# Building a scaled adjacency matrix quarter by quarter, with ScalarE's and VectorE's order in the first two pairs written anew

## The reference, cut to what matters

```
h    = relu(layernorm(x))                        # over the 1024 nodes
S    = normalised mean of h over the batch       # 1024 nodes x 128 features
sim  = (S S^T + 1) / 2
A    = (sim + g0 > 1 - sim + g1)                 # 1024 x 1024, zeros and ones
M    = clip(A + A^T + I, 0, 1);  C = M M^T       # common neighbours
W    = A * (C / max C * C)  where valid
deg  = W.sum(axis=0);  dinv = deg^-0.5 (0 where deg = 0)
Wn   = dinv[:,None] * W * dinv[None,:]
out  = x + (sum over s of Wn[s,d] * (h @ adj)[s]) + bias
```

## Time and profile before

| | us |
|---|---|
| median of 3 executions | 867.53 (867.31 to 867.67) |
| the profiled execution | 867.24 |
| its span, first to last instruction | 865.5 |
| TensorE busy with matmuls | 825.9 (95%) |
| VectorE busy | 582.5 (67%) |
| ScalarE busy | 507.1 (59%) |
| mean granted TensorE clock | 0.988 |

### The profile page before, as it was taken

The page is one execution under the profiler, slowest core; times in us unless marked ns, Lnnn a source line. Parts: engine busy times, 40 slices in busy tenths (PEclk is TensorE's granted clock), DMA queues, the critical chain, the costliest instruction groups (busy, mean ns, idle before and its releaser), DMA issues.

```text
span 865.5 us, 13587 instructions
## 1 busy us (share of the span) xinstructions
PE 825.9 (95%) x4771; PEld 431.2 (50%) x4778; DVE 582.5 (67%) x669; ACT 507.1 (59%) x522; POOL 314.8 (36%) x255
## 2 busy tenths in 40 slices
PE   4999999968899999999999999999999999999997
PEld 3544455544354555455545545555555455545553
DVE  7999987789846665666566556655665666566652
ACT  3888705877636664556456556656665655465531
POOL 4888810035004333433333333333333433333320
PEclk9999999997899999999999999999999999999999
DMA  8999903100643222222333333222222222222111
GB/s 334 409 410 357 421 13 122 49 1 1 236 154 98 98 98 98 98 97 97 97 126 108 111 111 125 98 97 97 97 97 97 97 97 97 97 97 98 60 63 73
DMA packets 30122, 113.15 MB, mean 131 GB/s; under 512 B 3472, under 2 KB 3600, under 8 KB 29072
## 3 DMA queue, kind: packets, MB, share of 16 engines
q1 hardware_dynamic: 30096, 112.80, 36.1%
HBM read 79.23 MB, written 33.55 MB: 130 GB/s over the span
## 4 chain that ended last, share of the span: by engine, by line
PE 77%; DVE 10%; issue 4%; ACT 4%; POOL 3%; DMA 0%; POOLq 0%; DVEq 0%; ACTq 0%; SPq 0%
PE ps L811 65%; PE ps L761 8%; DVE stats L903 4%; PE ps L779 1%; POOL rstd L335 1%; DVE a L1072 1%; DVE xring L1066 1%; POOL zbuf L345 1%; PE ps L690 1%; ACT zbuf L403 0%; ACT xring L574 0%; ACT a L579 0%; PE ps L704 0%; DVE moments L909 0%; ACT hring L454 0%
## 5 line engine op out<-in xcount | busy, mean ns | idle before, releaser
L811 PE MATMUL ps<-a,ybuf 128*128 128x512 f16 x2604 | 573.6, 380 | 3.4 <-ACT obuf L501 3.4
L811 PEld LDWEIGHTS ps<-a,ybuf 128*128 128x128 f16 x2604 | 253.2, 98 | 301.1 <-ACT obuf L501 3.9
L991 DVE TENSOR_TENSOR ybuf<-zbuf,ybuf 128x1024 f16<-128x1024 f32 x124 | 163.9, 1321 | 165.7 <-ACT ybuf L487 165.7
L371 POOL TENSOR_TENSOR zbuf<-zbuf 128x512 f32<-128x512 f32 x31 | 39.8, 1284 | 452.3 <-ACT zbuf L468 452.3
L487 ACT ACTIVATE ybuf<-zbuf 128x1024 f16<-128x1024 f32 x124 | 117.6, 950 | 110.4 <-POOL zbuf L376 97.2
L501 ACT ACTIVATE obuf<-ps,bias_sb,w_out 128x512 f32<-128x512 f32 x62 | 47.9, 773 | 126.6 <-PE ps L811 126.6
L980 DVE TENSOR_TENSOR hring<-hring 128x1024 f16<-128x1024 f32 x56 | 68.6, 1224 | 55.8 <-ACT hring L454 55.8
L761 PE MATMUL ps<-w,hring 128*128 128x128 f16 x1344 | 85.4, 221 | 11.6 <-DVE hring L980 9.8
L761 PEld LDWEIGHTS ps<-w,hring 128*128 128x128 f16 x1344 | 80.6, 99 | 24.8 <-DVE hring L980 10.1
L1138 DVE TENSOR_TENSOR obuf<-obuf,xring 128x1024 f32<-128x1024 f32 x64 | 78.3, 1225 | 2.7
L374 POOL TENSOR_TENSOR zbuf<-zbuf 128x512 f32<-128x512 f32 x31 | 70.4, 2271 | 0.0
(11 more groups left out here) (132 smaller groups left out, 675.0 us busy)
## 6 DMA issues: line engine op xcount, KB each, us to landing
xring<-in_x_dram SPq DMA_DIRECT2D x96, 512.0 KB, 4.7
out_dram<-obuf SPq DMA_DIRECT2D x64, 512.0 KB, 2.9
ybuf<-in_x_dram SPq DMA_DIRECT2D x28, 512.0 KB, 8.4
a<-in_L_gnn_gumbel_dram SPq DMA_DIRECT2D x7, 1024.0 KB, 14.7
obuf<-in_x_dram SPq DMA_DIRECT2D x11, 512.0 KB, 5.3
obuf<-in_L_gnn_gumbel_dram SPq DMA_DIRECT2D x1, 1024.0 KB, 22.7
w<-in_adj_dram SPq DMA_DIRECT2D x1, 64.0 KB, 1.8
bias_sb<-in_L_gnn_bias_dram SPq DMA_DIRECT2D x1, 0.5 KB, 2.2
```

Of the source, the lines that this page charges most:

```text
L811: mm = nc.tensor.matmul(bank[q % 2], y16[:, q % 2, yk, u, c * P:(c + 1) * P], a16[:, ak, mat, c, :], start=(start and c == yk == ak == 0), ...
L991: nc.vector.tensor_tensor(y16[:, q % 2, 1, a:a + n, :], z[:, a + 1:a + 1 + n, :], y16[:, q % 2, 0, a:a + n, :], ALU.subtract).then_inc(s_y, 1)
```

## The change

- `rooted` and `square` work on halves of 512 columns, 16 instructions each instead of 8 and 8, in the order of the quarters (rows_hi LO, rows_hi HI, rows_lo LO, rows_lo HI). ScalarE squares a quarter (4 instructions) and copies it at once; VectorE's `low` of a quarter stands behind the `rooted` of the next one.
- The bounds and roots of the degrees stand ahead of `y_low(0, 1, 2)`; `y_low(0, 1, 2)` and `y_low(0, 1, 3)` move behind the `low` of block 2. `relu2` is cut in its two activations, with `degree_of(7)` between those of entry 4.
- On TensorE q is spread in two halves, the first ahead of `turn(1)`. The fourteen `stay_awake` behind the last mask become five, and eight more stand behind the first block's `high`, ahead of the first product. `xw_of(0, 2, 1)` moves from there into pair 1, which now runs with its look-ahead.
- ScalarE's and VectorE's lists for pairs 0 and 1 are written out: the block results of pair 0 (`first_out`), `relu2(0, 3, 0)` and the work for pair 2 stand between the copies of the sums; `upper0(0, 1)` and `upper1(0, 1)` and two `y_low` stand ahead of pair 0's `add_x`.
- The masked counts lie in other slots of the matrix buffer.

```diff
-        masked = [tile16(e // 4, 5 + e // 2 % 2, e % 2) for e in range(C)]
+        masked = [tile16(half, mat, k) for half, mat in ((0, 5), (1, 5), (1, 3), (1, 4)) for k in (0, 1)]
...
             degree_of(6)
+            relu2_wide(0, 2, 0)
             degree_of(7)
+            relu2_high(0, 2, 0)
             y_high(0, 1, 3)
-            relu2(0, 2, 0)
...
+            def square(rows, k, half, c):
+
+                if k == 0 and half == 0 and c == 0:
+                    act.wait_ge(s_kap, 3)
+                act.wait_ge(s_e, C * k + HC * half + c + 1)
+                r = rows[:, c, half * H:(half + 1) * H]
+                nc.scalar.activation(r, r, ACT.Square, scale=kappa[:, 0:1]).then_inc(s_a32, 1)
...
+            for n, (mat, rows, k, half) in enumerate(((0, rows_hi, 0, 0), (A12, rows_hi, 0, 1),
+                                                      (1, rows_lo, 1, 0), (2, rows_lo, 1, 1))):
+                for c in range(HC):
+                    square(rows, k, half, c)
+                act.wait_ge(s_a32, HC * (n + 1))
+                high(mat, rows[:, :, half * H:(half + 1) * H])
             relu2(0, 2, 1)
...
             act.wait_ge(s_t, 1)
             high(3, spare)
+            act.wait_ge(s_wout, 1)
+            act.wait_ge(s_hhi, 5)
+            first_out(0)
+            relu2(0, 3, 0)
+            first_out(1)
+            z_of(0, 2, 0)
             act.wait_ge(s_t, 2)
             high(4, rows_hi[:, :, LO])
+            first_out(2)
+            first_out(3)
+            y_high(0, 2, 0)
+            act.wait_ge(s_hhi, 6)
+            partial(0, 1, 0)
             act.wait_ge(s_t, 3)
             high(5, rows_hi[:, :, HI])
-            relu2(0, 3, 0)
+            partial(0, 1, 1)
             act.wait_ge(s_t, 4)
             act.wait_ge(s_mm, 14 + 3)
             high(6, spare)
...
+            partial(0, 1, 2)
+            z_of(0, 2, 1)
+            y_high(0, 2, 1)
             relu2(0, 3, 1)
-            act.wait_ge(s_hhi, 7)
-            act_pair(0, 1, True, False, False)
+            y_high(0, 2, 2)
+            y_high(0, 2, 3)
...
             pe.wait_ge(s_m, C)
-            stay_awake(ps[:, 3, 0:P], 14)
-            turn(1)
-            spread(1)
+            stay_awake(ps[:, 3, 0:P], 5)
...
+            pe.wait_ge(s_adjt, C)
+            pe.wait_ge(s_q, 2)
+            q_row(0)
+            turn(1)
+            q_row(1)
+            spread(1)
             xw_of(0, 2, 0)
-            xw_of(0, 2, 1)
+            pe.wait_ge(s_ahi, 1)
+            stay_awake(ps[:, 3, 0:P], 8)
...
-                if ahead1:
+                if ahead1 and not second:
                     xw_of(i, q + 1, 0)
...
-            pe.wait_ge(s_e, C)
-            pe_pair(0, 1, False, True)
+            pe.wait_ge(s_e, 2 * C)
+            pe_pair(0, 1, True, True)
...
             mask(7)
-            y_low(0, 1, 2)
             root(0, 0, 6)
             bound(1, 6, C)
             root(1, 6, C)
...
+            h_low(0, 2, 0)
+            dve.wait_ge(s_qrow, 1)
+            rooted(rows_hi, 0, 0, 0)
             top_of(1)
-            y_low(0, 1, 3)
+            rooted(rows_hi, 0, 0, 1)
...
+            rooted(rows_hi, 0, 0, 2)
+            rooted(rows_hi, 0, 0, 3)
...
-            h_low(0, 2, 0)
             dve.wait_ge(s_qrow, 2)
             for c in range(HC):
-                rooted(rows_hi, 0, c)
+                rooted(rows_hi, 0, 1, c)
+            low(0, 0, rows_hi[:, :, LO])
             for c in range(HC):
-                rooted(rows_lo, 1, c)
+                rooted(rows_lo, 1, 0, c)
+            low(1, A12, rows_hi[:, :, HI])
+            for c in range(HC):
+                rooted(rows_lo, 1, 1, c)
+            low(2, 1, rows_lo[:, :, LO])
+            dve.wait_ge(s_a32, C)
+            nc.vector.tensor_tensor(spare, rows_hi[:, :, HI], rows_hi[:, :, LO], ALU.subtract).then_inc(s_t, 1)
+            low(3, 2, rows_lo[:, :, HI])
             h_low(0, 2, 1)
...
+            y_low(0, 1, 2)
+            y_low(0, 1, 3)
             dve.wait_ge(s_t, 1)
             dve.wait_ge(s_alo, 2)
             nc.vector.tensor_tensor(rows_hi[:, :, LO], rows_lo[:, :, HI], spare, ALU.subtract).then_inc(s_t, 1)
+            low(4, 3, spare)
+            low(5, 4, rows_hi[:, :, LO])
             nc.vector.tensor_tensor(rows_hi[:, :, HI], rows_lo[:, :, HI], rows_hi[:, :, HI],
                                     ALU.subtract).then_inc(s_t, 1)
-            low(4, 3, spare)
             dve.wait_ge(s_t, 2)
             dve.wait_ge(s_alo, 5)
             nc.vector.tensor_tensor(spare, rows_lo[:, :, LO], rows_hi[:, :, LO], ALU.subtract).then_inc(s_t, 1)
-            low(5, 4, rows_hi[:, :, LO])
+            h_low(0, 3, 0)
             low(6, 5, rows_hi[:, :, HI])
-            h_low(0, 3, 0)
             low(7, 6, spare)
...
+                if isinstance(i, int) and r == 1:
+                    dve.wait_ge(s_hhi, BODY - 1)
...
+            upper0(0, 1)
+            y_low(0, 2, 0)
+            upper1(0, 1)
+            y_low(0, 2, 1)
             add_x(0, 0, 0)
             add_x(0, 0, 1)
             h_low(0, 3, 1)
-            dve_pair(0, 1, True, False)
+            y_low(0, 2, 2)
+            lower0(0, 1)
+            add_x(0, 1, 0)
+            y_low(0, 2, 3)
+            lower1(0, 1)
+            add_x(0, 1, 1)
```

More of the change, by code:

```diff
@@ L432, in _, with relu2_wide @@
                                      accum_out=row_count[:, c:c + 1]).then_inc(s_mask[0], 1)
-            def relu2(i, q, b):
+            def relu2_wide(i, q, b):
                 i, q = i + q // PAIRS, q % PAIRS
                 j = 2 * q + b
-                if j == RESIDENT:
-                    return
                 n = (BODY - 1) * i + j - 1
@@ L451, in relu2, with relu2_high @@
                 t = BODY * i + j
-                bias, scale = nbias[:, bass.ds(t, 1)], rstd[:, bass.ds(t, 1)]
-                nc.scalar.activation(h32, src, ACT.Relu, bias=bias, scale=scale).then_inc(s_h32, 1)
-                nc.scalar.activation(h16[b][:, 0, :], src, ACT.Relu, bias=bias, scale=scale).then_inc(s_hhi, 1)
+                nc.scalar.activation(h32, src, ACT.Relu, bias=nbias[:, bass.ds(t, 1)],
+                                     scale=rstd[:, bass.ds(t, 1)]).then_inc(s_h32, 1)
+            def relu2_high(i, q, b):
+                i, q = i + q // PAIRS, q % PAIRS
+                j = 2 * q + b
+                first = isinstance(i, int) and i == 0 and j in x_first
+                src = x_first[j] if first else xring[:, j, :]
+                t = BODY * i + j
+                nc.scalar.activation(h16[b][:, 0, :], src, ACT.Relu, bias=nbias[:, bass.ds(t, 1)],
+                                     scale=rstd[:, bass.ds(t, 1)]).then_inc(s_hhi, 1)
+            def relu2(i, q, b):
+                if 2 * (q % PAIRS) + b != RESIDENT:
+                    relu2_wide(i, q, b)
+                    relu2_high(i, q, b)
             def z_of(i, q, b):
@@ L502, in partial, with act_pair @@
                                      scale=w_out[:, 0:1]).then_inc(s_v, 1)
-            def act_pair(i, q, ahead1, ahead2, evict=True):
+            def act_pair(i, q, ahead1, ahead2):
                 partial(i, q, 0)
                 if ahead1:
-                    if evict:
-                        z_of(i, q + 1, 0)
+                    z_of(i, q + 1, 0)
                     y_high(i, q + 1, 0)
@@ L514, in act_pair @@
                 if ahead1:
-                    if evict:
-                        z_of(i, q + 1, 1)
+                    z_of(i, q + 1, 1)
                     y_high(i, q + 1, 1)
@@ L577, in high @@
             def high(mat, src):
                 nc.scalar.activation(a16[:, 0, mat, :, :], src, ACT.Copy).then_inc(s_ahi, 1)
[L581 to L591, removed]
@@ L592, in _, with first_out @@
-            high(1, rows_lo[:, :, LO])
-            high(2, rows_lo[:, :, HI])
+            def first_out(n):
+                b, m, bank = FIRST_OUT[n]
+                act.wait_ge(s_mm, 14 + 4 + n)
+                nc.scalar.activation(o[0][b][:, m], bank, ACT.Identity, bias=bias_sb[:, 0:1],
+                                     scale=w_out[:, 0:1]).then_inc(s_first, 1)
+            for n, (mat, rows, k, half) in enumerate(((0, rows_hi, 0, 0), (A12, rows_hi, 0, 1),
[4 more added lines that the diff above has]
+                high(mat, rows[:, :, half * H:(half + 1) * H])
@@ L594, in _ @@
+            relu2(0, 2, 1)
             act.wait_ge(s_t, 1)
             high(3, spare)
+            act.wait_ge(s_wout, 1)
[4 more added lines that the diff above has]
+            z_of(0, 2, 0)
             act.wait_ge(s_t, 2)
             high(4, rows_hi[:, :, LO])
+            first_out(2)
[3 more added lines that the diff above has]
+            partial(0, 1, 0)
             act.wait_ge(s_t, 3)
@@ L793, in _, with q_row @@
             pe.wait_ge(s_m, C)
-            stay_awake(ps[:, 3, 0:P], 14)
-            turn(1)
-            spread(1)
-            pe.wait_ge(s_adjt, C)
-            for half in (0, 1):
```

(6 more changed lines are left out.)

12 lines of the change are left out of this document (removed).

## The result

The changed kernel takes 855.68 us (median of 4, 854.52 to 856.49) against 867.42 (4 executions) for the kernel before: ratio 0.9863, 95% interval 0.9846 to 0.9879, so 1.4% faster. 855.0 was predicted, 852.3 to 859.5 as the range. In a second group of runs it took 855.28 (4 executions, 853.56 to 856.10), the kernel before 867.63. The profiled execution is the fastest of the first four: 854.52, span 852.8, 12.7 less than before.

A forecast was written before the change was run, and what follows sets the result against it. TensorE, without a gap from 232.06, was taken as the bound: 7.0 at the start + 3.42 + 3.06 - 1.34 = 12.1, taken as 12.2, so 867.24 - 12.2 = 855.0 us; range 852.3 to 859.5.

The forecast's parts named there:

- Only the end of pair 1 counts: TensorE has no gap from 232.06 on, so the kernel's end moves exactly as pair 1's end, 248.07 to 235.8.
- Start of the path: From last mask to kappa: without y_low(0,1,2) ahead, roots end 0.9 us earlier and kappa ends at 186.2.
- The halves: rooted and square on 512 columns: steps of 0.67 and 0.61 us, from L1128 and ScalarE evictions, between half and full step.
- VectorE's list: Pairs 0 and 1: each low is at least 2.6 us ahead of TensorE's need; low 6 ends at 225.4.
- Rivals 2 and 4: VectorE becomes the bound, halves near full step: 860.7, chance 0.1; quarters late, four waits in pair 0: 881, chance 0.03.
- The wait of 3.42 and the clock's 3.06 behind it: Pair 1: TensorE's idling before 232.06 for a late partial, and the slow clock after it, both go.
- the clock's return: Ahead of the first product: clock down at 190.8, back at 195.8 to 196.7, effective start 195.6 against 202.58 before.
- rival 1: Clock does not fall at 190, or returns sooner; products start at 193.1, time 853.0, chance 0.22.
- The stores: Pair 2's first partial waits for pair 0's second store, ends at 241.4, asked for at 242.3: no loss, by 0.9 us.
- rival 3: Second store lands after 8.9 us, partial 3.6 late, clock may fall too: 858.6 to 861.7, chance 0.1.
- GpSimd's sums: GpSimd and VectorE take turns: up to 1.1 us on each of three or four VectorE instructions, no effect on the sum.

The follow-up runs named there:

- partials_late: Changed kernel with ScalarE's three partials of pair 1 moved back behind the copies of the last two sums: 860.08 us.
- awake_mask: Changed kernel with ten more zero matmuls on TensorE ahead of the wait for the last mask: 855.04 us.
- best: Changed kernel with more zero matmuls at both TensorE waits, pair 0's two stores ahead of the loads, and y_low(0,2,2) ahead of h_low(0,3,1): 853.70 us.
- best_sooner_stores: best with pair 0's two add_x sooner in VectorE's list: 852.68 us.
- after: The changed kernel without further edit, its first profiled execution: 854.52 us.
- after_again: The changed kernel measured again without edit: 855.28 us, its profiled execution 855.67.
- awake_through: Changed kernel with 24 zero matmuls, without the wait for the copy, instead of eight ahead of the first product: 854.44 us.
- stores_first: Changed kernel with the first trip's stores of entries 0 and 1 issued ahead of two x loads: 854.48 us.
- residue_first: Changed kernel with y_low(0,1,2) ahead of the roots again: 857.94 us, one execution 855.83.
- three_undone: Changed kernel with whole rows, late partials of pair 1 and y_low(0,1,2) ahead of the roots, all undone at once: 863.99 us.
- no_awake: Changed kernel without the eight zero matmuls and their wait ahead of the first product: 855.37 us.
- whole_rows: Changed kernel with rooted and square on whole rows of 1024 columns again, all rooted ahead of the lows: 858.60 us.

## Why the prediction was right, step by step

- **Only the end of pair 1 counts.** Right but for the stores: pair 1 ends 13.51 us earlier (247.91, now 234.40), 0.74 are lost behind it, and the span is 12.7 shorter.
- **Start of the path.** `kappa` 186.2 predicted, 186.10 measured. The `low` of block 0: 193.1 and 192.96.
- **The halves.** `rooted` 0.66 in the step (0.67 taken), four squares 2.56 (4 x 0.61 = 2.44). The near row, L1128, was the right one; neither bound was.
- **VectorE's list.** `low` 6 was forecast for 225.4 and ended at 224.80; no product of pairs 0 and 1 waited for any `low`. Rivals 2 and 4 are out.
- **The wait of 3.42 and the clock's 3.06 behind it.** Right, and reproduced by `partials_late` as 3.97 and 1.7: the idle part is the schedule's, the clock's part varies.
- **The term that was mis-sized: the clock's return.** It fell at 190.7, as taken (190.8), but I let it return 5.0 to 5.9 us after the restart, as in the earlier trace rows, to an effective start of 195.6. It returned after 3.4, just as the zeros ended, and the effective start was 194.2: 1.4 sooner. That is the second half of rival 1 ("or returns sooner"). In `awake_mask` it came back 5.7 us after the restart, as I had taken. What the two rows of before had in common was passed over: TensorE stood still for 5.3 and 0.9 us more after the clock had fallen, here it restarted as the clock fell (the last section has all falls). The Trainium skill's page "TensorE: Matmul & The Clock Gate" (What's actually happening) says that the gate's window does not start with the kernel and that the same kernel shows different numbers of slow matmuls; the runs agree: of two profiled executions of the changed kernel one spreads q at full clock and one at 1.2 GHz. I had weighed that rule down by three executions of the kernel before that lay within 0.36 us. The 31 that ran beside the experiments lie from 865.7 to 869.1: three were too few.
- **What I passed over.** I took the 2.51 us of idling before 181.33 as harmless, because the clock held in that one trace. In other executions it falls there, and the change has put the spreading of q (1.13, or 1.91 at half clock) straight on the path with only ten zeros ahead of it. That is the 1.1 us between the two profiled executions, and the medians (855.68, 855.28) lie above the profile that I forecast (854.52).
- **The stores (rival 3).** I gave them 0.9 us of slack with TensorE asking at 242.3. It asked at 240.9, and the `partial` ended at 241.6, against 241.4 forecast (the store took 5.3 us, not 4.3, but was issued at 235.5, not 236.2). The mechanism was there, at 0.7 us instead of 3.6. A sooner start is given back here until the stores come sooner: in `best` the start is 1.02 sooner and the gap 0.96, in `best_sooner_stores` there is no gap.
- **GpSimd's sums.** The sum of blocks that took 3.35 now takes 2.28 (216.97) with GpSimd idle, and two `add_x` beside GpSimd take 4.49 where before, with GpSimd idle, they took 2.35 (rows below). The reading of turns held, and with it the Trainium skill's page "SBUF — State Buffer" (Who interferes with whom). The `add_x` held up there are the ones behind which the stores are issued; they ended at 235.30, and the forecast had 235.9 for them.

VectorE's `add_x` of pair 0 in the kernel before, and GpSimd beside them in the changed one:

```profile
230.86 2.35 DVE L1138 TENSOR_TENSOR obuf<-obuf,xring 128x1024 f32<-128x1024 f32 x2
```

```profile
230.30 1.72 POOL L374 TENSOR_TENSOR zbuf<-zbuf 128x512 f32<-128x512 f32 x1
231.98 2.25 POOL L376 TENSOR_TENSOR zbuf<-zbuf 128x512 f32<-128x512 f32 x1
```

So 855.0 against 854.52 in the profiled execution is 1.4 too slow at the clock, 0.7 too fast at the stores, and the rest rounding. Term by term the sum had 7.0 for the start (8.4 measured: 7.15 and 1.22), 3.42 + 3.06 - 1.34 = 5.14 in pair 1 (5.14 measured) and 0 at the stores (-0.74 measured). That the two errors point opposite ways is luck; the 5.14 in pair 1 is not.

## What to carry to other kernels

When one engine has no gap from some point on, find that point in the trace before and after, and work out only its time; what other engines gain behind it is nothing. When a start moves forward, list what does not move with it (stores, loads, another engine's list), for it becomes the next wait: here three edits whose medians differed from the changed kernel's by 0.2 to 0.8 us, within its own spread, gave 1.6 together (with one `y_low` moved), and with pair 0's `add_x` moved too 2.6, which is clear of the spread. And judge a clock from many executions: a wait of 2.5 us may cost nothing in one and over 1 us in the next, and with two such waits filled with idle matmuls the spread was 0.3 us (`best`) and 0.1 (`best_sooner_stores`) instead of 2.5.

## What the runs showed of the hardware that was not expected

- TensorE's clock fell behind a wait of 2.51 us in five profiles (at 181.5 to 183.4) and held in five others with the same wait, the kernel before among them. Behind the waits of 3.8 us and more ahead of the first product it fell every time, between 189.6 and 193.8.
- How long it stayed at 1.2 GHz goes with what TensorE did after the fall, in all 17 falls between 181 and 232 us. Where it was at work, or restarted at most 0.4 us later, the clock was down for 3.4 us (all falls of `after`, `after_again`, `awake_through`, `stores_first`, `partials_late` and `residue_first`, and the first of `three_undone`). Where it stood still for 0.9 to 3.6 us more, it was down for 6.8 (`awake_mask` 1.1, `no_awake` 2.3, `three_undone` 2.7, `whole_rows` 3.6, and 0.9 in the kernel before at 231.2). Where it stood still for 5.3, in the kernel before at 193.6, it was down for 10.2. No run set out to test this.
- The second store of pair 0 (512 KB) took 3.9 to 6.6 us from issue to landing, with one load of the same size between it and the store before (nine profiles, seven of them 5.1 to 5.4), and 3.6 and 4.5 without that load (`stores_first`, `best`). In `best_sooner_stores`, issued 1.8 us sooner, it took 5.4, and the first of the two, issued at 229.2, 8.5.
